# A hybrid Mamba, expert and Performer block on one core: another order of the same operations on four engines

## The chip, the core and the metric

One core of one Trainium2 chip. TensorE (PE) multiplies matrices, VectorE (DVE), ScalarE (ACT) and GpSimd (POOL) work elementwise, SyncE (SP) issues the transfers. The metric is the time of one execution on the device, in microseconds (us); smaller is better.

## What is computed

Input x has 4 sequences of 1024 tokens with 256 features. Four stages follow each other, each a layer norm, a block and a residual addition. Cut to what matters:

```
x = x + mamba(layernorm(x))          # state s: 256 features x 32 numbers a sequence
    # s = clip(s * A + b_t * x_t, -10, 10);  y_t = sum(c_t * s);  1024 steps in a row
x = x + ffn(layernorm(x))            # 8 experts, relu, the two best weighted (FFN1)
x = x + performer_and_mlp(layernorm(x))   # causal linear attention, then a gelu MLP of 1024
x = x + ffn(layernorm(x))            # the same experts again (FFN2)
```

All of it is float32; the first layers of experts and MLP run as sums of products of a high and a low half.

## The kernel before

`front_part` makes the scan's operands for all tokens and is not touched. `main_part` then works in 16 chunks of 64 tokens a sequence. It is pipelined by hand: the function `step(i, c, late)`, which each engine has in a form of its own, does the scan of chunk i, and beside it Mamba's output, FFN1, attention and the start of the MLP for chunk c = i - 1, and the rest of the MLP and FFN2 for chunk late = i - 2. Each engine runs step(0), step(1), a loop over i = 2 to 15, and two steps that drain the pipeline, without a scan. An engine takes its work strictly in the order in which step calls it, and waits on semaphores. So the order of the calls is the schedule; no planner decides at run time.

The scan joins the engines. For each of 64 tokens ACT makes u(s) (line 928, `u_ring`, 8 slots: u(s) waits for scan step s - 8). DVE's scan_step multiplies the state by the decay (line 1626) and adds with clipping (line 1635), each in two halves; the state ring has 16 slots. PE's y(n) = scan_output(i, n) (line 1220) multiplies 8 finished states by `cblk`, which POOL's next_cblk fills (line 840); scan step 8n + 16 may not overwrite the ring before y(n).

Names that the prediction speaks of. PE: first_layer and mlp_first (line 1287, 12 products), second_layer and mlp_second (1300), tpose_set (1234, transposes; T_FFN1, T_ATT, T_WO, T_MLP, T_FFN2 name the set), features (1375), values (1382), turn_k (1397), scores (1408, 128 small products), from_states (1418), from_chunk (1428), new_states (1439), attention_out (1389), turn_y (the step's first transposes), mamba (1362). DVE: add_expert (1748), set_acc (1735), query_feature (1826), mask (1836), attended (1796 and 1799), add_states (1807), add_attention (1813), ln_stats (1659, 1662), low_half (1678), low_half_mlp (1684), gate_y (1760, the step's first work). ACT: relu (1035), gelu (1055), ln_apply (983), copy_set (992), copy_hi (1005), copy_comb (1042), spread_kv (1027), copy_y (1011). POOL: rstd_of (821 to 828), add_mlp_bias (872), add_attention (879). The last two are additions of 128x512 elements.

The end of a step is a chain: attention_out on PE, add_attention and ln_stats on DVE, add_attention and rstd_of on POOL, ln_apply on ACT, tpose_set(T_MLP) on PE, copy_hi on ACT, low_half_mlp on DVE, mlp_first on PE. The scan's end is another: the last scan step on DVE, y(7) on PE, copy_y on ACT, turn_y on PE, gate_y on DVE.

## Time and profile before

| | us |
|---|---|
| three runs, median (lowest to highest) | 1843.38 (1839.24 to 1846.09) |
| the profiled execution | 1845.13 |
| its span, first to last instruction | 1843.3 |
| PE busy (share) | 1693.8 (92%) |
| DVE busy | 1565.0 (85%) |
| ACT busy | 926.0 (50%) |
| POOL busy | 245.1 (13%) |

The profile is of one execution. What lies beside the span in it is 1.8 us. A busy PE counts matmuls whose ends are modelled, so a short wait can hide in a busy share; the starts of matmuls are exact. The text calls the stretch from one copy_y to the next a step.

### The profile page before, as it was taken

What the parts mean: (1) busy time and instruction counts of PE and PEld (TensorE: products, weight loads), DVE (VectorE), ACT (ScalarE), POOL (GpSimd) and SP (SyncE); (2) the same over time, 40 slices, a digit from 0 to 9 for tenths busy, and PEclk for the clock granted to TensorE, in tenths of its full rate; (3) what the DMA queues carried; (4) which work ended last, traced back from release to release, by engine and by line L of the source; (5) the groups of instructions that cost most, each with busy time, mean ns of one, the idle gap of its engine ahead of it and who ended that gap; (6) DMA issues with size and microseconds to landing.
All of it is one profiled execution on the core that took longest, in us unless ns stands there. A gap on an engine that the chain in (4) does not pass through costs nothing. (4 is left out here: it accounts for less than half of the span.)

```text
span 1843.3 us, 55933 instructions
## 1 busy us (share of the span) xinstructions
PE 1693.8 (92%) x16992; PEld 1422.4 (77%) x16992; DVE 1565.0 (85%) x5957; ACT 926.0 (50%) x2134; POOL 245.1 (13%) x515
## 2 busy tenths in 40 slices
PE   5774889999999999999999999999999999999987
PEld 3332668787887878787888878787878878787986
DVE  6589879899998989898999999898989999997522
ACT  4674445463645555554645555455536455554322
POOL 1011011111102011110102020111101020111000
PEclk9886879999999989998999999899989999999998
DMA  6885333242333333332433323332423333330000
GB/s 191 298 247 147 110 94 99 77 117 75 102 96 90 100 84 110 91 96 77 110 87 93 107 81 98 100 99 81 117 71 93 105 89 104 93 98 20 1 7 6
DMA packets 108425, 182.63 MB, mean 99 GB/s; under 512 B 45288, under 2 KB 71936, under 8 KB 107648
## 3 DMA queue, kind: packets, MB, share of 16 engines
q1 hardware_dynamic: 107232, 178.71, 33.9%
q8 instruction: 146, 2.39, 0.6%
q14 instruction: 119, 0.97, 0.2%
q10 hardware_dynamic: 928, 0.56, 0.1%
HBM read 161.35 MB, written 17.83 MB: 97 GB/s over the span
## 5 line engine op out<-in xcount | busy, mean ns | idle before, releaser
L1635 DVE CUSTOM_DVE_ANT_0 state<-decayed_state,u_ring 128x128 f32<-128x128 f32 x2048 | 522.3, 293 | 11.1 <-ACT u_ring L928 4.7
L1626 DVE TENSOR_TENSOR decayed_state<-state,decay 128x128 f32<-128x128 f32 x2048 | 508.1, 289 | 2.7 <-POOL m_rstd L813 1.2
L1300 PE MATMUL bank<-f_w_sb,hs_whole 128*128 128x256 f32 x2048 | 488.3, 382 | 0.6 <-DVE res L1748 0.6
L928 ACT ACTIVATE u_ring<-xrep,b_steps 128x256 f32<-128x256 f32 x1024 | 450.5, 503 | 52.5 <-DVE state L1635 46.0
L1300 PEld LDWEIGHTS bank<-f_w_sb,hs_whole 128*128 128x128 f32 x2048 | 374.2, 191 | 45.9 <-DVE res L1748 1.0
L1035 ACT ACTIVATE hs_whole<-bank,f_b_sb 128x256 f32<-128x256 f32 x512 | 214.1, 470 | 373.1 <-PE bank L1287 373.1
L1287 PE MATMUL bank<-late_fT_parts,f_w_hi 128*128 128x256 f32 x1024 | 187.6, 306 | 0.0
L1287 PE MATMUL bank<-fT_parts,f_w_hi 128*128 128x256 f32 x1024 | 179.5, 297 | 4.6 <-DVE fT_parts L1678 3.4
L1220 PE MATMUL bank<-state,cblk 128*32 128x256 f32 x2048 | 151.3, 423 | 16.4 <-DVE state L1635 16.4
L1287 PEld LDWEIGHTS bank<-fT_parts,f_w_hi 128*128 128x128 f32 x1024 | 142.5, 189 | 23.3 <-DVE fT_parts L1678 7.1
L1287 PEld LDWEIGHTS bank<-late_fT_parts,f_w_hi 128*128 128x128 f32 x1024 | 149.8, 194 | 11.8 <-issue 5.8
L1748 DVE SCALAR_TENSOR_TENSOR x<-bank,comb,x 128x256 f32<-128x256 f32 x256 | 111.6, 478 | 19.5 <-PE bank L1300 19.4
L1748 DVE SCALAR_TENSOR_TENSOR res<-bank,comb,res 128x256 f32<-128x256 f32 x256 | 111.7, 478 | 15.5 <-PE bank L1300 11.7
L1300 PE MATMUL bank<-m_w_sb,hs_whole 128*128 128x256 f32 x512 | 118.3, 379 | 0.0
L1220 PEld LDWEIGHTS bank<-state,cblk 128*32 128x32 f32 x2048 | 59.2, 117 | 75.4 <-issue 36.3
L1300 PEld LDWEIGHTS bank<-m_w_sb,hs_whole 128*128 128x128 f32 x512 | 94.9, 190 | 11.6
L879 POOL TENSOR_TENSOR mb<-mb,a_t 128x512 f32<-128x512 f32 x16 | 20.5, 1279 | 608.2 <-DVE a_t L1813 608.2
L992 ACT ACTIVATE turn<-bank 128x512 f32<-128x512 f32 x48 | 28.6, 595 | 136.5 <-PE bank L1234 136.5
L821 POOL TENSOR_TENSOR m_ve<-m_mv,m_eps 128x2 f32<-128x2 f32 x96 | 20.7, 216 | 562.7 <-DVE m_mv L1662 562.7
L1287 PE MATMUL bank<-late_fT_parts,m_w_hi 128*128 128x256 f32 x512 | 91.4, 301 | 0.0
L1287 PE MATMUL bank<-late_fT_parts,f_w_lo 128*128 128x256 f32 x512 | 83.1, 286 | 0.0
L1287 PE MATMUL bank<-fT_parts,f_w_lo 128*128 128x256 f32 x512 | 81.0, 281 | 0.0
(157 smaller groups left out, 2296.3 us busy)
## 6 DMA issues: line engine op xcount, KB each, us to landing
xrep<-xs_dram SPq DMA_DIRECT2D x1024, 128.0 KB, 2.6
xt<-in_x SPq DMA_DIRECT2D x4, 1024.0 KB, 7.7
xn_dram<-xn SPq DMA_DIRECT2D x4, 1024.0 KB, 5.6
xs_dram<-xs SPq DMA_DIRECT2D x8, 512.0 KB, 4.4
f_w_sb<-in_f_w SPq DMA_DIRECT2D x2, 2048.0 KB
z_dram<-zT SPq DMA_DIRECT2D x8, 512.0 KB, 4.5
z_t<-z_dram SPq DMA_DIRECT2D x64, 64.0 KB, 2.3
out<-x SPq DMA_DIRECT2D x64, 64.0 KB, 2.1
```

What stands on the lines that cost most here:

```text
L821: pool.tensor_tensor(ve[:, k], mv[:, k, :, 1], eps[:, k], ALU.add).then_inc(ve_done[k].sem, 1)
L879: pool.tensor_tensor(mb[:], mb[:], a_t[:], ALU.add).then_inc(mb_done.sem, 1)
L928: act.activation(u_ring[:, s % USLOTS], xrep[:, slot, n], ACT.Copy, scale=b_steps[:, s // BSTEPS, s % BSTEPS:s % BSTEPS + 1]).then_inc(u_m ...
L992: act.activation(whole[:].rearrange("p k q -> p (k q)"), (HB[1] if k == T_WO else TB)[:], ACT.Copy).then_inc(tcopied[k].sem, 1)
L1035: act.activation(hs_whole[:, e % 2, m], hidden_bank(c, f, e)[:, m * TOK:(m + 1) * TOK], ACT.Relu, bias=g["f_b1"][:, e, m:m + 1]).then_inc( ...
L1220: last = pe.matmul(Y[YCOLS * j:YCOLS * (j + 1), tile * D:(tile + 1) * D], cblk[:, slot * YCOLS:(slot + 1) * YCOLS], state[:, s % RING, :], ...
L1287: last = pe.matmul(dst(tile), *((w_, d_) if stationary == "w" else (d_, w_)), start=first and stationary != "more", stop=(n == len(PRODUCT ...
L1300: last = pe.matmul(bank_[:, tile * D:(tile + 1) * D], hs_whole[:, slot, m, tile * P:(tile + 1) * P], w(m), start=(m == 0 and tile == 0 and ...
L1626: dve.tensor_tensor(decayed_state[:, part], state[:, (s - 1) % RING, part], decay[:, part], ALU.mult).then_inc(decayed.sem, 1)
L1635: dve._custom_dve(add_sat, out=state[:, s % RING, part], in0=decayed_state[:, part], in1=u_ring[:, s % USLOTS, part], s0=LIMIT, s1=-LIMIT) ...
L1748: dve.scalar_tensor_tensor(out=dst[:, tile], in0=out_bank(c, f, e)[:, tile * D:(tile + 1) * D], scalar=comb[:, f, tile, e:e + 1], in1=dst[ ...
```

## The change

The diff moves calls and adds or removes none; every engine issues the same operations, SP's part is untouched. The functions themselves do not change. Its core, where "..." marks what is left out:

```diff
@@ POOL
                 add_to_tokens()
                 rstd_of(c, MAMBA)
                 rstd_of(c, FFN1)
+                rstd_of(late, FFN2)
+                rstd_of(c, OUTER)
+                add_mlp_bias()
                 next_cblk(0)
                 next_cblk(1)
-                rstd_of(late, FFN2)
+                rstd_of(c, LN1)
                 next_cblk(2)
-                rstd_of(c, OUTER)
-                add_mlp_bias()
                 next_cblk(3)
-                rstd_of(c, LN1)
                 next_cblk(4)
+                next_cblk(5)
                 add_attention()
                 rstd_of(c, LN2)
-                next_cblk(5)
                 next_cblk(6)
@@ ACT
                 u(2)
                 u(3)
                 u(4)
+                gelu(late, 1)
                 u(5)
                 u(6)
                 u(7)
-                gelu(late, 1)
                 u(8)
                 u(9)
+                gelu(late, 2)
                 u(10)
+                gelu(late, 3)
                 u(11)
-                gelu(late, 2)
-                u(12)
-                gelu(late, 3)
                 ln_apply(c, FFN1, res, turn, xf_done[0])
                 copy_hi(c, T_FFN1)
                 copy_set(c, T_FFN1)
+                u(12)
                 u(13)
                 u(14)
+                u(15)
                 relu(c, 0, 0)
-                u(15)
+                u(16)
                 relu(c, 0, 1)
                 copy_comb(c, 0)
-                u(16)
-                relu(c, 0, 2)
                 u(17)
                 u(18)
                 u(19)
                 ln_apply(late, FFN2, x3, late_turn, xf_done[1])
...
                 u(48)
                 u(49)
                 u(50)
                 u(51)
-                relu(late, 1, 6)
                 u(52)
                 u(53)
                 u(54)
...
                 u(58)
                 u(59)
+                relu(late, 1, 6)
                 u(60)
+                spread_kv(c)
                 u(61)
                 u(62)
+                u(63)
                 relu(late, 1, 7)
                 ln_apply(c, LN2, a_t, late_turn, yl_done)
-                u(63)
-                spread_kv(c)
                 copy_hi(c, T_MLP)
@@ PE
                 first_layer(c, 0, 1)
                 if_both(x3_done, late, 1)
                 second_layer(c, 0, 0)
-                first_layer(c, 0, 2)
                 turn_comb(c, 0)
                 second_layer(c, 0, 1)
                 bias(c, 0)
-                y(1)
-                first_layer(c, 0, 3)
+                first_layer(c, 0, 2)
                 if_both(acc_set[0], c, 1)
                 tpose_set(late, T_FFN2, xf_done[1])
+                first_layer(c, 0, 3)
                 second_layer(c, 0, 2)
                 gate(late, 1)
+                second_layer(c, 0, 3)
                 first_layer(c, 0, 4)
-                second_layer(c, 0, 3)
+                y(1)
                 first_layer(c, 0, 5)
                 second_layer(c, 0, 4)
+                first_layer(c, 0, 6)
+                second_layer(c, 0, 5)
                 turn_comb(late, 1)
-                second_layer(c, 0, 5)
-                first_layer(c, 0, 6)
-                bias(late, 1)
                 first_layer(c, 0, 7)
                 second_layer(c, 0, 6)
+                second_layer(c, 0, 7)
                 if_both(relued[0], c, F // P * (E - 1))
                 first_layer(late, 1, 0)
-                second_layer(c, 0, 7)
+                y(2)
+                if_both(acc_done[0], c, TILES * (E - 1))
+                second_layer(late, 1, 0)
                 if_both(relued[0], c, F // P * E)
                 first_layer(late, 1, 1)
-                if_both(acc_done[0], c, TILES * (E - 1))
-                second_layer(late, 1, 0)
-                y(2)
-                y(3)
+                bias(late, 1)
                 first_layer(late, 1, 2)
                 if_both(acc_done[0], c, TILES * E)
                 second_layer(late, 1, 1)
+                y(3)
                 first_layer(late, 1, 3)
                 second_layer(late, 1, 2)
                 if_both(acc_set[1], late, 1)
                 tpose_set(c, T_ATT, xl_done)
                 second_layer(late, 1, 3)
-                first_layer(late, 1, 4)
                 if_both(relued[1], late, F // P * 2)
                 pe.wait_ge(tcopied[T_ATT].sem, tcopied[T_ATT].after(c, 1))
                 features(g["wk"], k_made)
-                second_layer(late, 1, 4)
-                first_layer(late, 1, 5)
                 values()
-                pe.wait_ge(kT_done.sem, kT_done.after(c, 1))
-                features(g["wq"], q_made)
+                first_layer(late, 1, 4)
                 pe.wait_ge(kT_done.sem, kT_done.after(c, 1))
                 pe.wait_ge(v_copied.sem, v_copied.after(c, TILES))
                 turn_k()
+                pe.wait_ge(kT_done.sem, kT_done.after(c, 1))
+                features(g["wq"], q_made)
+                second_layer(late, 1, 4)
+                first_layer(late, 1, 5)
                 y(4)
                 pe.wait_ge(qT_done.sem, qT_done.after(c, 2))
                 pe.wait_ge(k_copied.sem, k_copied.after(c, 1))
...
                 pe.wait_ge(masked.sem, masked.after(c, 3))
                 pe.wait_ge(kv_set.sem, kv_set.after(c, 0))
                 from_states()
+                y(5)
                 wait_apart(masked, masked.after(c, GH))
                 from_chunk(0)
                 from_chunk(1).then_inc(num_made.sem, 1)
                 new_states(0).then_inc(kv_half.sem, 1)
+                tpose_set(c, T_WO, at_done, HB[1])
                 wait_apart(kv_half, kv_half.after(c, 1))
                 new_states(1).then_inc(kv_made.sem, 1)
-                tpose_set(c, T_WO, at_done, HB[1])
-                y(5)
                 pe.wait_ge(tcopied[T_WO].sem, tcopied[T_WO].after(c, 1))
                 attention_out()
                 second_layer(late, 1, 6)
                 first_layer(late, 1, 7)
                 y(6)
+                second_layer(late, 1, 7)
                 pe.wait_ge(kv_added.sem, kv_added.after(c, 1))
                 tpose_set(c, T_MLP, yl_done)
-                second_layer(late, 1, 7)
                 y(OCTS - 1)
                 if late is not None:
                     pe.wait_ge(relued[1].sem, relued[1].after(late, E * (F // P)))
@@ DVE
                         first_layer_low(n)
                 mamba_norm()
                 ln_stats(c, FFN1, res, x1_done, (1, 2))
-                scan(5, 11)
+                scan(5, 10)
+                add_mlp()
                 if c is not None and late is None:
                     mlp_low()
                 low_half(c, T_FFN1)
-                add_mlp()
+                ln_stats(late, FFN2, x3, x3_done, (1, 1))
+                scan(10, 11)
+                routing(c, 0)
                 scan(11, 14)
-                routing(c, 0)
-                ln_stats(late, FFN2, x3, x3_done, (1, 1))
-                scan(14, 16)
                 set_acc(c, 0, res, res)
-                scan(16, 17)
+                scan(14, 15)
                 add_expert(c, 0, 0, res)
+                scan(15, 17)
+                add_expert(c, 0, 1, res)
                 scan(17, 18)
-                add_expert(c, 0, 1, res)
-                scan(18, 19)
                 add_expert(c, 0, 2, res)
+                scan(18, 21)
                 routing(late, 1)
-                scan(19, 22)
+                scan(21, 22)
                 add_expert(c, 0, 3, res)
-                scan(22, 23)
+                scan(22, 27)
                 add_expert(c, 0, 4, res)
-                scan(23, 25)
                 low_half(late, T_FFN2)
-                scan(25, 29)
                 add_expert(c, 0, 5, res)
+                scan(27, 28)
+                add_expert(c, 0, 6, res)
+                scan(28, 29)
+                add_expert(c, 0, 7, res)
                 scan(29, 30)
-                add_expert(c, 0, 6, res)
-                scan(30, 31)
-                add_expert(c, 0, 7, res)
                 ln_stats(c, OUTER, res, acc_done[0], (TILES * (E - 1) + 1, TILES * E))
-                scan(31, 32)
+                scan(30, 32)
+                ln_apply(c, OUTER, res, a_t, a_done)
+                scan(32, 33)
                 set_acc(late, 1, x3, x3)
-                ln_apply(c, OUTER, res, a_t, a_done)
+                scan(33, 34)
                 ln_stats(c, LN1, a_t, a_done, (1, 2))
-                scan(32, 35)
+                scan(34, 35)
                 add_expert(late, 1, 0, x3)
                 ln_affine(LN1, a_t, "ln1_s", lambda tile: rows["ln1_b"][:], turn, xl_done)
                 add_expert(late, 1, 1, x3)
                 scan(35, 37)
                 add_expert(late, 1, 2, x3)
-                scan(37, 38)
+                scan(37, 39)
                 add_expert(late, 1, 3, x3)
-                scan(38, 42)
+                scan(39, 40)
                 key_feature()
-                scan(42, 43)
-                add_expert(late, 1, 4, x3)
-                scan(43, 44)
+                scan(40, 44)
                 query_feature(0)
                 query_feature(1)
-                scan(44, 46)
+                scan(44, 45)
+                add_expert(late, 1, 4, x3)
+                scan(45, 47)
                 mask(0)
+                scan(47, 48)
                 mask(1)
                 mask(2)
-                scan(46, 47)
+                scan(48, 50)
                 mask(3)
-                scan(47, 51)
+                scan(50, 53)
                 add_expert(late, 1, 5, x3)
+                scan(53, 54)
                 attended()
-                scan(51, 57)
+                scan(54, 59)
                 add_states()
-                scan(57, 59)
+                scan(59, 60)
                 add_attention()
+                scan(60, 61)
                 ln_stats(c, LN2, a_t, xr_done, (1, 1))
-                scan(59, 61)
                 add_expert(late, 1, 6, x3)
                 scan(61, 64)
+                add_expert(late, 1, 7, x3)
                 low_half_mlp()
-                add_expert(late, 1, 7, x3)
 
             step(0, None, None)
             step(1, 0, None)
```

Three places in the order of the instructions. The first is PE's queue in the loop, from from_states (line 1418) to attention_out (1389); 1439 is new_states, 1234 the transposes T_WO, 1220 a y. Before:

```order
L1418 MATMUL bank<-kv,qT 64x68 x16
L1428 MATMUL bank<-vv,ss 64x17 x64
L1439 MATMUL bank<-vv,ktok 32x17 x64
L1234 MATMUL bank<-ident_sb,turn 128x128 x4
L1214 REGISTER_ALU
L1215 REGISTER_ALU
L1220 MATMUL bank<-state,cblk 32x256 x8
L1389 MATMUL bank<-wo_sb,turn 128x256 x4
```

and now:

```order
L1418 MATMUL bank<-kv,qT 64x68 x16
L1214 REGISTER_ALU
L1215 REGISTER_ALU
L1220 MATMUL bank<-state,cblk 32x256 x8
L1428 MATMUL bank<-vv,ss 64x17 x64
L1439 MATMUL bank<-vv,ktok 32x17 x32
L1234 MATMUL bank<-ident_sb,turn 128x128 x4
L1439 MATMUL bank<-vv,ktok 32x17 x32
L1389 MATMUL bank<-wo_sb,turn 128x256 x4
```

y(5) has moved ahead of from_chunk, and the transposes of the attended values stand between the two halves of new_states.

The second is PE's queue at the end of the loop's body, from y(6) to y(7). Before:

```order
L1220 MATMUL bank<-state,cblk 32x256 x8
L1234 MATMUL bank<-ident_sb,late_turn 128x128 x4
L1321 REGISTER_ALU
L1322 REGISTER_ALU
L1300 MATMUL bank<-f_w_sb,hs_whole 128x256 x4
L1214 REGISTER_ALU
L1215 REGISTER_ALU
L1220 MATMUL bank<-state,cblk 32x256 x8
```

and now:

```order
L1220 MATMUL bank<-state,cblk 32x256 x8
L1321 REGISTER_ALU
L1322 REGISTER_ALU
L1300 MATMUL bank<-f_w_sb,hs_whole 128x256 x4
L1234 MATMUL bank<-ident_sb,late_turn 128x128 x4
L1214 REGISTER_ALU
L1215 REGISTER_ALU
L1220 MATMUL bank<-state,cblk 32x256 x8
```

The last expert's second layer now stands ahead of the transposes T_MLP, not behind them.

The third is ACT's queue at the end of step(1), which has the loop's order without the work of the late chunk. From T_WO's copy (992) on, 928 is u, 983 ln_apply, 1027 spread_kv, 1005 copy_hi, 1011 copy_y. Before:

```order
L992 ACTIVATE turn<-bank 128x512
L928 ACTIVATE u_ring<-xrep,b_steps 128x256 x6
L983 ACTIVATE late_turn<-a_t,m_shift,m_rstd 128x256 x2
L928 ACTIVATE u_ring<-xrep,b_steps 128x256
L1027 ACTIVATE kv<-kv_sum 32x16x17 x4
L1005 ACTIVATE late_fT_parts<-bank 128x512
L1011 ACTIVATE turn<-bank 128x512
```

and now:

```order
L992 ACTIVATE turn<-bank 128x512
L928 ACTIVATE u_ring<-xrep,b_steps 128x256 x4
L1027 ACTIVATE kv<-kv_sum 32x16x17 x4
L928 ACTIVATE u_ring<-xrep,b_steps 128x256 x3
L983 ACTIVATE late_turn<-a_t,m_shift,m_rstd 128x256 x2
L1005 ACTIVATE late_fT_parts<-bank 128x512
L1011 ACTIVATE turn<-bank 128x512
```

spread_kv has left its place between the normed rows and their high halves, and the last u stands ahead of ln_apply.

## Rows read from the trace of the kernel before

**Rows 1.** The page: span, busy time of each engine, a DMA queue (packets, MB, share)

```profile
span 1843.3 us, 55933 instructions
PE 1693.8 (92%) x16992; PEld 1422.4 (77%) x16992; DVE 1565.0 (85%) x5957; ACT 926.0 (50%) x2134; POOL 245.1 (13%) x515
...
q8 instruction: 146, 2.39, 0.6%
```

**Rows 2.** Busy time by window: stretch, length, engines, granted clock (PEclk), DMA

```profile
158.70:261.50 102.80, 71.76 (x781) 55.85 (x781) 89.80 (x337) 43.59 (x100) 14.46 (x26) 0.73 0.34 91
261.50:1690.40 1428.90, 1382.53 (x14505) 1190.27 (x14506) 1312.32 (x5095) 746.23 (x1780) 202.87 (x420) 0.96 0.33 93
1690.40:1843.30 152.90, 133.80 (x1164) 121.39 (x1164) 53.86 (x142) 40.20 (x92) 12.83 (x26) 0.93 0.03 7
1388.50:1489.00 100.50, 97.13 (x1037) 83.61 (x1038) 93.83 (x365) 53.33 (x128) 14.52 (x30) 0.98 0.36 97
1077.90:1182.90 105.00, 100.33 (x1037) 86.11 (x1038) 93.93 (x365) 53.13 (x128) 14.43 (x30) 0.95 0.32 92
...
1474.00:1480.80 6.80, 6.80 (x41) 4.73 (x38) 6.48 (x30) 2.99 (x7) 0.00 (x0) 0.75 0.28 83
```

**Rows 3.** Timeline of PE, end of the step at 1388.5: start, length, instructions, [idle before]

```profile
1468.14 3.91 PE L1428 MATMUL bank<-vv,ss 64*64 64x17 f32 x128
...
1473.97 1.10 PE L1234 MATMUL bank<-ident_sb,turn 128*128 128x128 f32 x4
1475.00 1.94 PE L1220 MATMUL bank<-state,cblk 128*32 128x256 f32 x16
1476.87 2.26 PE L1389 MATMUL bank<-wo_sb,turn 128*128 128x256 f32 x8
1478.96 1.89 PE L1300 MATMUL bank<-f_w_sb,hs_whole 128*128 128x256 f32 x8
...
1482.20 1.07 PE L1220 MATMUL bank<-state,cblk 128*32 128x256 f32 x16
1485.53 0.63 PE L1234 MATMUL bank<-ident_sb,late_turn 128*128 128x128 f32 x4 [2.26 <-ACT late_turn L983]
```

**Rows 4.** Timeline of DVE, end of the same step

```profile
1472.11 0.37 DVE L1796 RECIPROCAL rec<-bank 128x16 f32<-128x16 f32 x2 [0.85 <-PE bank L1428]
...
1473.07 0.48 DVE L1626 TENSOR_TENSOR decayed_state<-state,decay 128x128 f32<-128x128 f32 x2
...
1476.40 0.49 DVE L1626 TENSOR_TENSOR decayed_state<-state,decay 128x128 f32<-128x128 f32 x2
...
1478.03 0.50 DVE L1635 CUSTOM_DVE_ANT_0 state<-decayed_state,u_ring 128x128 f32<-128x128 f32 x2 [0.32 <-DVE decayed_state L1626]
...
1480.46 0.68 DVE L1813 TENSOR_TENSOR a_t<-bank,a_t 128x512 f32<-128x512 f32 x1
...
1482.15 0.80 DVE L1626 TENSOR_TENSOR decayed_state<-state,decay 128x128 f32<-128x128 f32 x2
...
1488.14 0.69 DVE L1684 TENSOR_TENSOR late_fT_parts<-bank,late_fT_parts 128x512 fp32r<-128x512 f32 x1 [0.66 <-ACT late_fT_parts L1005]
...
1491.09 1.31 DVE L1760 TENSOR_TENSOR z_t<-bank,z_t 128x128 f32<-128x128 f32 x4 [1.47 <-PE bank L1234]
```

**Rows 5.** Timeline of POOL and ACT, the same stretch

```profile
1481.31 1.28 POOL L879 TENSOR_TENSOR mb<-mb,a_t 128x512 f32<-128x512 f32 x1 [37.02 <-DVE a_t L1813]
...
1485.69 1.80 ACT L1027 ACTIVATE kv<-kv_sum 32x272 f32<-32x272 f32 x4
```

**Rows 6.** Timeline of PE and DVE, two waits earlier in that step

```profile
1406.78 0.74 PE L1287 MATMUL bank<-fT_parts,f_w_hi 128*128 128x256 f32 x4 [0.34 <-DVE fT_parts L1678]
...
1460.53 1.53 DVE L1826 TENSOR_SCALAR qT<-bank,feature_floor_sb,feature_eps_sb 128x512 f32<-128x512 f32 x2 [1.42 <-PE bank L1375]
```

**Rows 7.** Timeline of PE in scores and behind them, step at 1077.9

```profile
1155.43 0.44 PE L1408 MATMUL bank<-qT,kT 32*64 32x64 f32 x18 [2.46 <-issue]
...
1157.91 2.92 PE L1300 MATMUL bank<-f_w_sb,hs_whole 128*128 128x256 f32 x8
```

More of the change, by code:

```diff
@@ L1108, in step @@
                 ln_apply(late, FFN2, x3, late_turn, xf_done[1])
+                relu(c, 0, 2)
                 copy_set(late, T_FFN2)
@@ L1115, in step @@
                 u(23)
+                relu(c, 0, 5)
                 u(24)
-                relu(c, 0, 5)
-                copy_comb(late, 1)
                 u(25)
                 u(26)
-                copy_hi(late, T_FFN2)
                 u(27)
@@ L1125, in step @@
                 u(29)
+                copy_hi(late, T_FFN2)
+                copy_comb(late, 1)
                 u(30)
+                u(31)
                 relu(c, 0, 7)
-                u(31)
                 u(32)
+                relu(late, 1, 0)
                 u(33)
-                relu(late, 1, 0)
                 u(34)
@@ L1137, in step @@
                 u(38)
+                u(39)
                 relu(late, 1, 2)
-                u(39)
                 u(40)
+                u(41)
                 relu(late, 1, 3)
+                u(42)
                 copy_set(c, T_ATT)
-                u(41)
-                u(42)
                 u(43)
+                copy_v(c)
                 u(44)
                 relu(late, 1, 4)
-                copy_v(c)
+                copy_k(c)
                 u(45)
                 u(46)
+                u(47)
                 relu(late, 1, 5)
-                copy_k(c)
-                u(47)
                 u(48)
```

## The prediction

> **What bounds the kernel now.** I read the page first, then the windows by step, then the timelines of one step. The page has PE busy for 92% of the span and DVE for 85% [rows 1], which does not yet say which of them decides. The windows do: the 14 steps from 261.5 to 1690.4 take 1428.9 us, 102.06 each, and PE is busy in 1382.5 of these, DVE in 1312.3 [rows 2]. Two engines are nearly full, so a step is as long as the work of either plus the waits that they cause each other. The step at 1388.5 takes 100.5, that at 1077.9 takes 105.0 [rows 2]; four of the 14 are like the second (104.1 to 105.0), ten like the first (100.3 to 102.3). The 4.5 us between the two come out of rows 7, to which I return. Step 1 before the loop and the drain behind it, 102.8 and 152.9 us, are not like this: PE is busy in 71.8 of the first, DVE in 53.9 of the second [rows 2].
>
> In the timeline of the shorter kind PE waits 2.26 us for T_MLP's rows behind y(6), and 0.34 for the low half in the first expert layer [rows 3, 6]. DVE waits 1.42 in query_feature, 0.85 in attended, 0.32 in the scan step behind it that needs y(5)'s place in the ring, 0.66 in low_half_mlp, 1.47 in gate_y [rows 4, 6]. From 1474.0 to 1480.8 the granted clock averages 0.75 [rows 2], full speed in one half and 1.2 GHz in the other: y(5) takes 1.94 in it, y(6) behind it 1.07 [rows 3]. Ahead of that PE did scores, from_states and from_chunk, hundreds of products of 17 to 68 columns.
>
> **The change, part by part.** Nothing is added or removed, and neither SP nor any DMA moves; ACT and POOL are busy for half and an eighth of the time [rows 1]. So only waits can change, and what runs beside what. I cost one loop step and multiply by 14.
>
> *The middle of the step, up to attended.* On DVE the scan steps 51 to 53 go ahead of attended. A scan step costs 0.83 (four from 1473.07 to 1476.40 [rows 4]), so 2.5 us of work go where DVE idled 1.42 + 0.85 = 2.27. On PE, y(5) goes ahead of from_chunk, 1.0 at full clock, while the 0.34 wait goes, since low_half runs a scan step earlier with add_mlp (0.6) in its place, and the small wait of scores for the queries goes, since k and q now come ahead of two expert layers. PE has the experts' layers to work on there, and I find no new wait over a few tenths: each second_layer's bank was freed by an add_expert that DVE reaches in time. So attended starts within half a microsecond of where it was; I book 0 for the middle. What would hurt is scores becoming later; then mask(0) waits on DVE.
>
> *The end on DVE.* From the first scan step behind attended to gate_y it is 1473.07 to 1491.09, 18.0 us [rows 4]. Three scan steps go, -2.5. The wait of 0.32 goes, since y(5) is long done. The wait of 0.66 goes: copy_hi stood behind spread_kv's 1.80 on ACT [rows 5] and now does not, and add_expert(7) fills the time. Against it stands POOL: its add_attention runs 1.28 us from 1481.31 [rows 5], and the pair of L1626 that starts beside it takes 0.80 where its neighbour takes 0.48 [rows 4]. It now has scan(60, 61) beside it from its first moment, where it had ln_stats. I charge the whole 1.28 less the 0.32 paid already, +0.96, as the row shows the DVE pair ending only with POOL's; the other end is 0. Sum: -2.5 - 0.32 - 0.66 + 0.96 = -2.5. gate_y's own wait of 1.47 stays, since y(7), copy_y and turn_y still follow the last scan step.
>
> The Trainium skill ("SBUF — State Buffer", section "SBUF: two separate sides") has GpSimd and a VectorE operation with two SBUF inputs share one port pair as an exclusive lock, with the loser blocked for the whole instruction. It speaks against this change, and L1626's 0.80 agrees with it. Without that rule this part would be -3.5 a step.
>
> *The end on PE.* From from_chunk's end (1468.14 + 3.91) to turn_y the same stretch of 18 us holds y(5) and the wait of 2.26. y(5) leaves: -1.9 here, +1.0 in the middle. second_layer(late, 1, 7), some 1.7 long, now covers the wait: -1.7. The first layer's 0.34 goes too. Sum: -2.9. But where y(5) and waits lay under the half clock, attention_out and second_layer(6) now come. At the slow clock a second_layer takes 2.92 instead of 1.89 [rows 3, 7], so each of the two may cost 1.0 more: between -0.9 and -2.9.
>
> *The step.* Both chains must come round, so the later one counts. DVE's is -2.5, PE's -0.9 to -2.9. I take **-2.4**, near DVE's, as attention_out was partly under the slow clock already (2.26 for the work of 1.89). 14 x 2.4 = 33.6. In step 1 PE has room and DVE's end gains the same waits, but it is one step: 0 to 2.5, I take 0. In the drain there is no scan, PE is busy in 133.8 of 152.9 and orders of experts change nothing: 0. The profiled execution took 1845.1; 1845.1 - 33.6 = 1811.5. The median of the three runs is 1.7 lower, so **1810**.
>
> **The longer steps.** In the step at 1077.9 scores stops after 110 of its 128 products for 2.46 us, "issue": no semaphore was awaited. Behind it products run at the slow clock [rows 7]. Queue q8 carried 146 packets, 2.39 MB, 16 KB each [rows 1]; that is 9 or 10 in a step, and PE has some 2075 products and weight loads in one [rows 2]. I read this as loading of code: scores issues 256 instructions in 1.5 us. The number and kind of instructions ahead of scores in the loop is unchanged, with y(4) still just ahead, so the block border falls at the same product; I leave four such steps as they are. The Trainium skill ("Runtime: NRT & Kernel Launch", section "Instruction fetch mechanics") has such blocks of 16 KiB mostly hidden, the next being fetched during the current one. By that no step would be long, before or after; the row of 2.46 says otherwise.
>
> **The rivals.**
> - *Dense and unstalled.* The clock's slow stretch falls no worse than before, the port costs nothing, and chance lets the stops of scores go away: -3.3 x 14 = -46, and four times 4.5 = -18 more. That is 1779; with half of the stops 1788. The waits in the rows speak for it, the four long steps against it. Its near end is 1797.
> - *The slow clock eats the gain.* It lasts longer, as work with few columns (from_states, y(5), from_chunk, new_states, transposes) now stands closer together, and attention_out, second_layer(6) and first_layer(7) all run slow. Then PE gains 0.3 a step or so: 1843.4 - 4 = 1839. For it: clock 0.75 in the same place; against it: y(5), which has 256 columns a product, comes into the thin stretch.
> - *Scores stops in every step: slower.* The place is between y(4) and scores. The queries now come earlier, so scores follows y(4) without its small wait, and there are a few tenths less for the code to arrive. Each stop costs 4.5, and up to 5.4 where no wait behind it (part of the 2.26) takes it up. Without stops the time would be 1843.4 - 18 - 34 = 1792; with 14 of them at 5.4, 1868. It decides from about 10 of 14 steps on (10 x 5.4 = 54 against the 52 of both gains). For it: the stop exists; against it: ten steps of 14 don't have it, with the same code.
> - *The change doesn't do what it says*: the three places of the order show that it does; no chance of its own.
>
> **How the numbers follow.** Forecast 0.68, its own range 1797 to 1829 (3.3 and 1.0 a step). Dense and unstalled 0.10, slow clock 0.12, stops in every step 0.10. A measurement of this kernel can tell about 0.5%, 9 us, from no change. Faster: 0.68 + 0.10 = 0.78; within: 0.12; slower: 0.10. The range goes from 1788, half of the stops gone, to 1846, the slow clock with a few more stops; it leaves out the last rival and a piece of the first.
>
> **What would show it.** Steps of 97.5 to 98.5 us between copies of y, four or so longer; idle PE before the T_MLP transposes under 0.5; no wait in low_half_mlp; no wait of 1.42 in query_feature, and instead up to 1 us before the first mask; POOL's L879 with a long L1626 beside it. It is wrong if from_chunk ends over 1 us later in the step than 83.6, if L1408 shows an issue wait in most steps, or if the clock is slow for over 7 us behind from_chunk.

## Result and the profile after

The changed kernel takes 1817.18 us (median of 4 runs, 1816.62 to 1818.00), against 1843.72 before: ratio 0.986, 95% interval 0.984 to 0.988. That is 7 us above the forecast of 1810 and inside its range. The page:

```profile
span 1814.9 us, 55933 instructions
PE 1689.0 (93%) x16992; PEld 1416.7 (78%) x16992; DVE 1580.4 (87%) x5957; ACT 933.3 (51%) x2134; POOL 246.6 (14%) x515
```

The windows of step 1, of the 14 loop steps, of the drain and of the ordinary step at 1065.5, to set beside [rows 2]; the columns are the same:

```profile
159.50:267.50 108.00, 72.40 (x781) 56.29 (x782) 90.73 (x337) 44.63 (x100) 14.25 (x26) 0.72 0.31 87
267.50:1663.60 1396.10, 1377.25 (x14505) 1184.83 (x14506) 1326.76 (x5096) 752.30 (x1779) 204.62 (x420) 0.97 0.34 95
1663.60:1814.90 151.30, 133.11 (x1164) 120.70 (x1164) 53.62 (x141) 40.41 (x92) 12.82 (x26) 0.95 0.03 7
1065.50:1165.30 99.80, 98.88 (x1037) 85.00 (x1038) 94.90 (x365) 53.72 (x128) 14.62 (x30) 0.97 0.35 97
```

The loop gives 1428.9 - 1396.1 = 32.8, nearly the 33.6 of the forecast, but not from where the forecast had it. Ordinary steps went from 100.5 to 99.7, only 0.8 and not 2.4. Here 100.5 is an undisturbed step of before, like those at 977.4 and 1388.5; the median over its ten steps without a stop is 100.8, and against that it is 1.1. The long steps of 104 to 105 are gone: the longest of the 14 is the first, 100.5, all others lie within 99.5 to 99.9. Step 1 grew from 102.8 to 108.0.

That the long steps are gone shows in what PE's idle time in front of scores' products and their weight loads was put down to. The changed kernel (us, times), where the 5.8 are 0.41 ahead of the first product of each loop step and none is inside scores:

```profile
  issue: 5.8, 14
  DVE qT L1826: 1.7, 2
```

and the kernel before, same view:

```profile
  issue: 29.6, 23
  DVE qT L1826: 7.2, 18
```

PE's timeline of the step at 1065.5, from scores to turn_y, beside [rows 3]:

```profile
1139.17 1.59 PE L1408 MATMUL bank<-qT,kT 32*64 32x64 f32 x128
...
1145.13 1.07 PE L1220 MATMUL bank<-state,cblk 128*32 128x256 f32 x16
1146.14 3.91 PE L1428 MATMUL bank<-vv,ss 64*64 64x17 f32 x128
...
1153.23 3.78 PE L1389 MATMUL bank<-wo_sb,turn 128*128 128x256 f32 x8
1156.81 2.08 PE L1300 MATMUL bank<-f_w_sb,hs_whole 128*128 128x256 f32 x8
...
1160.21 1.07 PE L1220 MATMUL bank<-state,cblk 128*32 128x256 f32 x16
1161.60 1.99 PE L1300 MATMUL bank<-f_w_sb,hs_whole 128*128 128x256 f32 x8 [0.33 <-DVE x L1748]
1163.43 0.61 PE L1234 MATMUL bank<-ident_sb,late_turn 128*128 128x128 f32 x4
```

y(5) takes 1.07 at the full clock where it took 1.94 at the half, and the wait of 2.26 for T_MLP's rows is gone. attention_out takes 3.78 where it took 2.26: the granted clock is 0.50 from 1150.40 to 1157.20.

```profile
1150.40:1157.20 6.80, 6.43 (x112) 5.19 (x102) 6.31 (x29) 3.97 (x10) 0.00 (x0) 0.50 0.24 72
```

The same step on DVE, from the last mask to gate_y, and POOL's add_attention beside it:

```profile
1145.11 0.68 DVE L1836 TENSOR_TENSOR ss<-bank,causal_sb 128x512 f32<-128x512 f32 x1
...
1150.10 0.37 DVE L1796 RECIPROCAL rec<-bank 128x16 f32<-128x16 f32 x2 [0.20 <-PE bank L1428]
...
1153.55 0.49 DVE L1635 CUSTOM_DVE_ANT_0 state<-decayed_state,u_ring 128x128 f32<-128x128 f32 x2 [0.34 <-ACT u_ring L928]
...
1158.07 1.57 DVE L1635 CUSTOM_DVE_ANT_0 state<-decayed_state,u_ring 128x128 f32<-128x128 f32 x2
...
1164.76 0.68 DVE L1684 TENSOR_TENSOR late_fT_parts<-bank,late_fT_parts 128x512 fp32r<-128x512 f32 x1
1167.39 1.01 DVE L1760 TENSOR_TENSOR z_t<-bank,z_t 128x128 f32<-128x128 f32 x3 [1.95 <-PE bank L1234]
```

```profile
1157.91 1.38 POOL L879 TENSOR_TENSOR mb<-mb,a_t 128x512 f32<-128x512 f32 x1 [18.09 <-DVE a_t L1813]
```

The pair of L1635 takes 1.57 beside POOL, where a pair takes 0.51. The waits in low_half_mlp (0.66) and in query_feature (1.42) are gone, gate_y's grew from 1.47 to 1.95.

**A way to cut a step.** For the experiments a step is cut at attended (L1796): from copy_y to attended, and the rest up to the next copy_y. All times but the last two columns count from the step's first copy_y. The rows are medians over the 14 loop steps, here and in the table further down, except that before has its undisturbed steps (977.4 and 1388.5):

| kernel | scores starts | attended | rest | step |
|---|---|---|---|---|
| before | 73.7 | 83.6 | 16.85 | 100.5 |
| changed | 73.7 | 84.6 | 14.90 | 99.7 |

So the new end gives 1.95 and the way up to attended takes 1.0 of it back. Against the medians of before's ten steps without a stop (attended 83.9, step 100.8) the way up to attended takes 0.7.

### The profile page after: what moved, and what is told of

The parts are those of the page before. It is cut to its first block and busy times, and to the rows that moved or that the text cites. A ratio compares the mean times of both kernels' runs of the same rounds, so it can differ in the third digit from the quotient of the medians.

```text
span 1814.9 us, 55933 instructions
## 1 busy us (share of the span) xinstructions
PE 1689.0 (93%) x16992; PEld 1416.7 (78%) x16992; DVE 1580.4 (87%) x5957; ACT 933.3 (51%) x2134; POOL 246.6 (14%) x515
## 5 line engine op out<-in xcount | busy, mean ns | idle before, releaser
L1635 DVE CUSTOM_DVE_ANT_0 state<-decayed_state,u_ring 128x128 f32<-128x128 f32 x2048 | 552.9, 308 | 18.2 <-ACT u_ring L928 10.5
L1287 PE MATMUL bank<-late_fT_parts,f_w_hi 128*128 128x256 f32 x1024 | 181.1, 299 | 0.1
L1220 PE MATMUL bank<-state,cblk 128*32 128x256 f32 x2048 | 142.2, 396 | 19.3 <-DVE state L1635 13.7
L1287 PEld LDWEIGHTS bank<-late_fT_parts,f_w_hi 128*128 128x128 f32 x1024 | 145.3, 190 | 11.1 <-issue 5.8
L1748 DVE SCALAR_TENSOR_TENSOR res<-bank,comb,res 128x256 f32<-128x256 f32 x256 | 111.5, 478 | 11.0 <-PE bank L1300 10.2
L1220 PEld LDWEIGHTS bank<-state,cblk 128*32 128x32 f32 x2048 | 54.9, 111 | 67.9 <-issue 26.7
L1055 ACT ACTIVATE hs_whole<-bank,m_b_sb 128x256 f32<-128x256 f32 x128 | 53.5, 469 | 77.6 <-PE bank L1287 77.6
```

The lines of the kernel that those rows point to most:

```text
L1055: act.activation(hs_whole[:, j % 2, m], HB[j % 2][:, m * TOK:(m + 1) * TOK], ACT.Gelu_apprx_tanh, bias=g["m_b1"][:, 2 * j + m:2 * j + m + ...
L1220: last = pe.matmul(Y[YCOLS * j:YCOLS * (j + 1), tile * D:(tile + 1) * D], cblk[:, slot * YCOLS:(slot + 1) * YCOLS], state[:, s % RING, :], ...
L1287: last = pe.matmul(dst(tile), *((w_, d_) if stationary == "w" else (d_, w_)), start=first and stationary != "more", stop=(n == len(PRODUCT ...
L1635: dve._custom_dve(add_sat, out=state[:, s % RING, part], in0=decayed_state[:, part], in1=u_ring[:, s % USLOTS, part], s0=LIMIT, s1=-LIMIT) ...
L1748: dve.scalar_tensor_tensor(out=dst[:, tile], in0=out_bank(c, f, e)[:, tile * D:(tile + 1) * D], scalar=comb[:, f, tile, e:e + 1], in1=dst[ ...
```

## Experiments

There are twelve kernels in three groups: e1 to e4; r1 and e5 to e7; e8 to e11. Before ran beside each group: 1833.68 (1824.62 to 1849.44, 23 runs), 1848.12 (1842.79 to 1860.40, 7) and 1842.97 (1831.67 to 1859.03, 19). It scatters by over 1%, the changed kernel by 0.1%; so totals are compared within a group, and where the text goes across groups it says so. Steps are compared by their profiles, one execution of each kernel.

### The parts of the change alone

e1: middle on PE (and its counterparts on DVE and ACT, copy_k ahead of relu(5)); before:

```diff
-                first_layer(late, 1, 4)
...
                 features(g["wk"], k_made)
-                second_layer(late, 1, 4)
-                first_layer(late, 1, 5)
                 values()
...
-                features(g["wq"], q_made)
+                first_layer(late, 1, 4)
...
                 turn_k()
...
+                features(g["wq"], q_made)
+                second_layer(late, 1, 4)
+                first_layer(late, 1, 5)
                 y(4)
```

> The kernel before with the middle of the new order alone: on PE the queries' features, second_layer(4) and first_layer(5) stand between turn_k and y(4), on DVE the queries come ahead of add_expert(4) and scan steps stand between the masks, on ACT copy_k comes ahead of relu(5). Theory A: the long steps come from code that arrives too late behind y(4); with an expert's two layers ahead of y(4) PE's fetch starts over 1 us earlier relative to scores, so no step has an issue wait in L1408, and ordinary steps keep 100.5, since scores starts where it did (PE bound). Total 1843.4 - 4 x 4.5 - some 2 for the smaller ones = 1823 to 1826. Rival B: the stops come and go by chance or hang on the end of the step; then three or more long steps of 104 to 105 remain and the time is 1839 to 1846.

e2: the end, from from_states on, as in the diff of the change.

> The kernel before with the end of the new order alone: y(5) ahead of from_chunk, T_WO between the halves of new_states, second_layer(7) ahead of T_MLP, scan steps 51 to 53 ahead of attended, (60) beside POOL's add_attention, add_expert(7) ahead of low_half_mlp, and ACT's and POOL's moves that go with them. Theory A: ordinary steps fall from 100.5 to 99.6 (attended 0.95 later because of y(5), the end 1.8 shorter), the long steps stay, four or so, step 1 grows by 2 to 5: 1843.4 - 12 + 3 = 1834. Rival B: it is the end that takes the long steps away: 1816 to 1820.

e3: both.

> Middle and end together; against the changed kernel only the head of the step (up to the transposes T_ATT) stays as before. Theory A: the head is worth nothing, so 1817 +- 3, with no long step, ordinary steps of 99.6 and step 1 near 108. Rival: the head gives the part that the other two do not, 1823 or more here.

e8: e1 with the masks together:

```diff
                 mask(0)
-                scan(47, 48)
                 mask(1)
                 mask(2)
-                scan(48, 50)
+                scan(47, 48)
                 mask(3)
-                scan(50, 51)
+                scan(48, 51)
```

> The kernel before with the middle of e1, but the masks together again (0, 1, 2, one scan step, 3). Theory A: e1 lost 1.0 a step because mask(3) comes 1.3 later and from_chunk waits for it, and gained the stops; so here attended is back near 83.3, ordinary steps 100.0 to 100.4, no stop inside scores: 1843 - 18 - 4 and, with step 1, about 1822 to 1828. Rival B: e1's loss is the thin work at the half clock that begins earlier; then ordinary steps stay over 101 and the time near 1838.

| kernel | median us (runs) | steps stopped in scores | scores | attended | rest | step |
|---|---|---|---|---|---|---|
| e1 middle | 1843.42 (10) | 0 of 14 | 73.3 | 84.8 | 16.85 | 101.5 |
| e2 end | 1828.17 (10) | 1 | 73.6 | 85.2 | 14.90 | 100.2 |
| e3 both | 1809.79 (4) | 0 | 73.3 | 84.2 | 14.90 | 99.3 |
| e8 middle, masks together | 1823.89 (4) | 0 | 73.2 | 83.2 | 16.85 | 100.3 |

Against before beside them, e1 is 10 us slower, e2 6 and e3 24 faster, and e8 is 19 faster.

Three readings. The rest is 16.85 wherever the old end stands and 14.90 wherever the new one does: the end's gain adds up. The stops go with the middle: none in e1, e3 and e8. In e2's profile one is left, at the same product as in [rows 7]:

```profile
1341.36 1.44 PE L1408 MATMUL bank<-qT,kT 32*64 32x64 f32 x110 [0.26 <-DVE qT L1826]
1345.53 0.68 PE L1408 MATMUL bank<-qT,kT 32*64 32x64 f32 x18 [2.73 <-issue]
```

And the middle alone is no gain in total (1843): it takes the stops away but attended comes 1.2 later. My expectation of e1 was wrong by 18 us there, though right on the stops. The reason stands in its timeline: the scan steps between the masks make mask(3) late, and from_chunk waits 0.74. The granted clock then averages 0.82 from 1060.90 to 1065.50, and from_chunk takes 4.57 instead of 3.91.

```profile
1059.00 1.17 PE L1418 MATMUL bank<-kv,qT 128*64 128x68 f32 x32
1060.90 4.57 PE L1428 MATMUL bank<-vv,ss 64*64 64x17 f32 x128 [0.74 <-DVE ss L1836]
```

e8 confirms it: with the masks together from_chunk starts 0.8 earlier in the step than in e1 and, at the faster clock, ends 1.6 earlier; attended is at 83.2, and the total 20 us less (in another group). In the loop windows e3 is 5.2 us below the changed kernel, and it has the old head, so the head of the new order gains nothing and costs about 0.35 a step (scores at 73.3 against 73.7). e5 and e7, further down, differ by this head alone, within one group: 1813.85 with it, 1805.46 without.

```profile
267.56:1658.50 1390.94, 1368.27 (x14505) 1185.19 (x14506) 1322.69 (x5096) 750.77 (x1779) 205.02 (x420) 0.97 0.34 96
```

### What y(5) ahead of from_chunk does

```diff
                 from_states()
-                y(5)
                 wait_apart(masked, masked.after(c, GH))
                 from_chunk(0)
                 from_chunk(1).then_inc(num_made.sem, 1)
+                y(5)
                 new_states(0).then_inc(kv_half.sem, 1)
```

> The changed kernel with y(5) moved back behind from_chunk, one call. Theory A: y(5) fills the wait for mask(3) (0.74 in e1) at the full clock; behind from_chunk it runs at the half clock (1.87 instead of 1.00) and on the way to T_WO, attended is at most 0.3 earlier: ordinary steps 100.4 to 101.0, total 1828 to 1836. Rival B: y(5) ahead of from_chunk is a plain delay of 1.0 on the way to attended, as its 84.55 against 83.60 looks; then each step gets shorter by 0.5 to 1.0 and the total is 1803 to 1810.

e9 takes 1838.69 (1836.32 to 1840.75, 10 runs), with steps of 101.7 and some of 100.3; the changed kernel, in the group before, takes 1817.16. That is theory A's direction, some 3 us beyond its end; rival B is out. The rows show both halves of it, the wait and the half clock, which here lasts 10.2 us and in the changed kernel's loop steps at most 6.8:

```profile
1057.59 4.20 PE L1428 MATMUL bank<-vv,ss 64*64 64x17 f32 x128 [0.73 <-DVE ss L1836]
1061.71 1.93 PE L1220 MATMUL bank<-state,cblk 128*32 128x256 f32 x16
```

```profile
1061.00:1071.20 10.20, 10.20 (x176) 7.59 (x174) 7.87 (x34) 5.39 (x13) 0.00 (x0) 0.50 0.21 54
```

Attended is even 0.3 later without y(5) in front. With the masks spaced as here, y(5) is not a delay of 1.0; it fills a wait that the spacing makes. Where they stand together it is one: in e2 the last mask ends 78.6 into the step, as in before, and from_chunk starts at 80.6 instead of 79.6. So two things hold from_chunk back to 80.6 in the changed kernel, and either would do nearly all of it: y(5), and a last mask that ends at 80.3. Masks together and y(5) behind from_chunk, with the rest of the new end, was not run.

### Where the stops in scores come from

e4 and e10 leave work and order of before as they are and shift code. At the top of the loop body:

```diff
+                if late is not None:
+                    for _ in range(40):
+                        pe.wait_ge(pool_set.sem, POOL_SETS)
                 turn_y()
```

> The kernel before, with 40 waits on a semaphore that has long had its value at the top of PE's loop body: work and order the same, but PE's code from there on lies 40 instructions further back. Theory A (code arrival): the place where scores stopped moves 20 products forward, to about product 90, and the fetch for what lies behind it is asked for 40 instructions earlier in the work, over 1 us earlier; the long steps go, 1823 to 1828 if the 40 waits cost nothing (they may cost up to 1 us a step, up to 14 more). Rival B (the stop belongs to scores itself or to chance): products stop at 110 as before, four long steps.

and the same with 16 waits on DVE ahead of gate_y:

> The kernel before with 16 waits that are long satisfied at the top of DVE's loop body, where DVE waits for PE anyway: the code of DVE lies 16 instructions further back. It tells what makes PE's fetch come 2.5 late in some steps. Rival C (a clash of the two fetches: in every step of before another queue's fetch lands at 71.4, 0.7 ahead of PE's at 72.1): with that one shifted no step stops, all times of the kernel within 1822 to 1827. Theory A (PE's own lead alone): stops as in before, its times as far apart as those of before, up to 1845.

e4 takes 1854.73 (8 runs), e10 1844.96 (1828.35 to 1854.89, 10 runs). In e4 no loop step stops, neither behind 110 products nor behind 90; its 40 waits cost 1.7 a step, more than I had allowed, so its total says nothing for the theory and its trace does. In e10 seven of 14 steps stop, behind 110 products each, though the fetch of the other queue (q14) moved from 71.4 to 70.3: rival C is out.

```profile
1158.90 1.44 PE L1408 MATMUL bank<-qT,kT 32*64 32x64 f32 x110 [0.26 <-DVE qT L1826]
1162.80 0.68 PE L1408 MATMUL bank<-qT,kT 32*64 32x64 f32 x18 [2.46 <-issue]
```

The packets of queue q8 tell the rest. In ordinary steps of before (the loop's first left out) one starts 72.0 to 72.3 into the step, 1.5 ahead of scores. In the stopping step at 1077.9 there is none; the transfers from 1149.90 to 1152.40 (72.0 to 74.5 into the step), then from 1152.40 to 1153.00:

```profile
DMA packets 0, 0.00 MB, mean 0 GB/s; under 512 B 0, under 2 KB 0, under 8 KB 0
```

```profile
q8 instruction: 1, 0.02, 16.2%
```

It starts at 74.6, when scores is at work already. Where an expert's layers stand ahead of y(4), as in e1 (its window 1051.00 to 1052.00 holds the packet, at 70.7), it starts 2.5 ahead of scores:

```profile
q8 instruction: 1, 0.02, 7.0%
```

| | fetch starts ahead of scores, typically | loop steps that stopped |
|---|---|---|
| before, e2, e10 | 1.5 | 4, 1 and 7 of 14 each |
| changed, e1, e3, e5 to e9, e11 | 2.5 | 0 of 140 with the repeat of the changed kernel |
| e4 | 6.5 | 0 of 14 |

The typical value is that of steps without a stop. In the second line two steps have a lead of only 1.7, and they don't stop either.

So a stop goes with a late fetch, and the lead is set by what stands ahead of y(4) (e1) or by where the code lies (e4). That q8 brings PE's code is inferred from this. Why the fetch with the short lead starts 2.5 later in some steps and not in others stays open; no run tells it. The Trainium skill ("Runtime: NRT & Kernel Launch", section "Instruction fetch mechanics") has the next block fetched while the current one runs, mostly hidden. In scores that holds for the 154 steps of the last two lines and not for 12 of 42 in the first.

### The port

```diff
                 add_attention()
-                scan(60, 61)
                 ln_stats(c, LN2, a_t, xr_done, (1, 1))
+                scan(60, 61)
                 add_expert(late, 1, 6, x3)
```

> The changed kernel with DVE's ln_stats(LN2) ahead of scan step 60 again, one swap. Theory A (port): the pair beside POOL's add_attention no longer waits it out (1.89 to 0.83 for the step, some 0.3 stays as in before), and LN2's mean comes 1.9 earlier, so T_MLP too: 0.5 to 0.8 a step, 7 to 11 below the changed kernel. Rival B: PE sets the end of the step, what DVE saves is waited for at gate_y: within 2 of the changed kernel.

e6 takes 1806.07 (1802.65 to 1807.10, 4 runs), against 1817.16 of the changed kernel beside it: 11 less, and 0.69 a step (rest 14.46, step 99.0). The pair beside POOL now takes 0.81, and second_layer(7) stands behind y(6) without a wait:

```profile
1053.74 0.81 DVE L1626 TENSOR_TENSOR decayed_state<-state,decay 128x128 f32<-128x128 f32 x2
```

```profile
1055.09 1.07 PE L1220 MATMUL bank<-state,cblk 128*32 128x256 f32 x16
1056.09 1.99 PE L1300 MATMUL bank<-f_w_sb,hs_whole 128*128 128x256 f32 x8
```

This is theory A, at the upper end of its size; PE did not hold the gain back.

### Step 1, and all together

r1 is the changed kernel again, e5 the changed kernel with this in all four engines' step functions, where the first branch holds the body in the order of before, the second the new one:

```diff
+                if late is None:
...
+                else:
...
```

> The changed kernel itself again, as the measure for the three beside it. Both theories: 1817 +- 3, no issue wait inside scores in any loop step, PE's fetch at 71.0 and scores at 73.65 in the step.

> The changed kernel with step(0) and step(1), which have no late chunk, in the order of before on all four engines; the loop and the drain as changed. Theory A: step 1 is a chain of latencies with idle engines, and y(5) ahead of from_chunk, the scan steps between the masks and (60, 61) lie on that chain: step 1 falls from 107.9 to 102.8 and the stretch ahead of it by 0.8, total 5 to 6 below the changed kernel. Rival: step 1's growth comes from the head of the loop's first step or from the clock and only moves; the sum of step 1 and step 2 falls by less than 2.

> Middle and end of the new order in the loop and drain, the head as before, and step(0) and step(1) all as before. Additive: the run with middle and end (1809.8) less 5 to 6: 1804. Rival: the head of the changed kernel is worth as much as on a par, then no lower than e5.

> What the runs point to, together: middle and end of the new order, head as before, step(0) and step(1) as before, ln_stats(LN2) ahead of scan step 60. Additive from e7 (1805.5) and e6 (-0.66 a step, -11 in all): 1795 to 1797, ordinary steps 98.6. Rival: the two gains meet at PE, whose own work then fills the step: 1801 or more.

r1 takes 1817.16, e5 1813.85, e7 1805.46 and e11 1800.02 (4 runs each, none more than 3.1 from its median). e5 is 3.3 below r1, and e7 4.3 below e3 (in another group): the direction of theory A, two thirds of its size. Step 1 of one kernel isn't constant: it takes 108.0 in the first profile of the changed kernel, 105.2 in the second; 102.8 in before's, and 105.2 in e10's, whose step 1 is before's; 104.6 in e5's. What e5 and e7 lack of the forecast lies in scores at least in part: in step 1 it stops for 1.4 and 1.7, 116 products in. before's profile has no such stop; those of e4, e10 and e11, with the same step 1, have it. In before's the fetch starts 1.4 ahead of scores there, in these five 0.5 behind its start. So step 1 shows the same as the loop. PE is at rest for a third of step 1. As the changed kernel has it:

```profile
240.37 2.08 PE L1418 MATMUL bank<-kv,qT 128*64 128x68 f32 x32 [3.54 <-DVE ss L1836]
242.38 1.94 PE L1220 MATMUL bank<-state,cblk 128*32 128x256 f32 x16
244.24 7.01 PE L1428 MATMUL bank<-vv,ss 64*64 64x17 f32 x128
...
264.45 1.09 PE L1234 MATMUL bank<-ident_sb,late_turn 128*128 128x128 f32 x4 [6.22 <-ACT late_turn L983]
```

and as before had it:

```profile
236.42 1.17 PE L1418 MATMUL bank<-kv,qT 128*64 128x68 f32 x32 [1.98 <-DVE ss L1836]
237.94 6.67 PE L1428 MATMUL bank<-vv,ss 64*64 64x17 f32 x128 [0.36 <-DVE ss L1836]
```

Here the scan steps between the masks (a wait of 3.54 for the mask instead of 1.98), and y(5) at the half clock, stand ahead of from_chunk with no other work to hide them. e11 is the best version: 0.977 of before (0.970 to 0.985), 17 us below the changed kernel of the group before. It misses the additive 1796 by 4: ordinary steps are 98.9, not 98.6. PE is busy in 1373.8 of the loop's 1384.2, so the rival (the gains meet at PE) may have a share in it; no run shows that.

```profile
263.99:1648.16 1384.17, 1373.82 (x14505) 1190.72 (x14506) 1312.33 (x5096) 750.35 (x1780) 209.00 (x420) 0.97 0.34 96
```

## Why the prediction was right, and where not

The total was right, and in part by luck: the ordinary steps gave 11 us of the 34 booked, and steps that the forecast left as they are gave 22. Each part in turn:

- **The middle, booked at 0: wrong.** Attended comes 1.0 later. The 0.34 and the wait of scores for the queries did go, but scores starts at 73.7 as before (the head costs 0.35). So nothing paid for y(5)'s 1.0 ahead of from_chunk, and the masks with scan steps between them end 1.7 later, which alone would hold from_chunk back nearly as long. I had looked for a later scores, not for a later mask(3); the second is what e1 showed.
- **The end on DVE, -2.5: from the first scan step behind attended to gate_y it went from 18.0 to 16.3, -1.7.** Three scan steps left it, as booked. The 0.66 went. The port cost the pair 1.57 - 0.51 = 1.06, where the forecast had 1.28; less the 0.32 that before paid already it is 0.74, against the 0.96 of the forecast. So the rule of the Trainium skill ("SBUF — State Buffer", "SBUF: two separate sides") held, and e6, which got 0.69 a step back, agrees with the size. The 0.32 did not go, and I had read it wrongly: it stands ahead of scan step 56 in both kernels (median 0.32 in each), though in the changed one y(5) was done 7 us before it, and u(56), which ACT makes ahead of T_WO's copy, 8.6 us before it. So it isn't y(5)'s, nor u's, though the view puts it down to u_ring; its cause stays open (ACT's rows stand below). And gate_y's wait, "stays", grew by 0.5: without it DVE's stretch got 2.2 shorter, and PE's, which turn_y ends, only 1.7.
- **The end on PE, -0.9 to -2.9: at its weak end.** That sum holds y(5)'s +1.0 in the middle and the 0.34 of the head. From from_chunk's end to turn_y it went from 18.3 to 16.6, -1.7; with these two it is -1.0. In the two steps shown, by the starts of the groups: y(5) -1.9, y(6) with the wait behind it -1.9; against that, at the half clock, attention_out +1.5 and second_layer(6) +0.2, and new_states and T_MLP +0.2 each. I had allowed up to 1.0 for each of attention_out and second_layer(6), and together they took 1.7 of the 2.0. "The later one counts", I wrote, and then took DVE's -2.4, for which PE would have had to come near its good end. The step shortened by 1.95 (copy to copy) less 1.0.
- **The four long steps, "left as they are": wrong.** They took 104.7 on average, 17 us above four undisturbed ones; together with smaller hitches of the other steps of before, which are gone too and which no run explains, it is 21.8. I argued that the number of instructions ahead of scores had not changed, so neither had the block border. The number is indeed the same, 1055 from turn_y to scores in both traces; where the border falls can't be seen where nothing stops. But what counts is how long before scores PE reaches the place at which the fetch is asked for, and the two expert layers put there made that 1.0 more. I had even written, as a rival, that less time would be left for the code; it is more.
- **Step 1, 0 to a gain of 2.5: wrong in sign**, +5.2 between the two profiles, 3 to 4 by e5 and e7. Drain: 1.6 less, booked at 0.
- Of the rivals, the stops of scores went away as in the first one, but not by chance: 0 of 140. The slow clock, the second, took most of what the forecast had allowed it. The run's signs: no wait in low_half_mlp, none in query_feature, none of PE ahead of T_MLP, a wait of 0.41 before the first mask and the long pair beside L879 came as written; steps of 97.5 to 98.5 did not. from_chunk ends 84.56 into the step (median), just short of the mark that I had set for being wrong (84.6), and the half clock behind it lasts up to 6.8 us, just short of the 7 that I had set.

In us: ordinary shortening 14 x 0.8 = 11, the stops and smaller hitches of the other steps 21.8, step 1 -5.2, front and drain +0.8: 28.4 between the two spans.

ACT's rows in the step at 1065.5 for u(56) and, next in its queue, T_WO's copy; the wait of scan step 56 ends at 1153.55:

```profile
1144.39 0.51 ACT L928 ACTIVATE u_ring<-xrep,b_steps 128x256 f32<-128x256 f32 x1 [1.52 <-DVE state L1635]
1152.36 0.60 ACT L992 ACTIVATE turn<-bank 128x512 f32<-128x512 f32 x1 [7.46 <-PE bank L1234]
```

## What to carry to other kernels

Count what an order does to the slowest chain in the prologue too: an order that fills a full loop with other work delays the stages that have none to fill with. A burst of many small instructions needs its code early, and longer work ahead of it gave it here 1 us more; in a trace, compare where the fetch starts, not only how many instructions there are. And when single steps of a loop are longer than the rest, find their cause before pricing a change at the ordinary step.

## Not expected of the hardware

- A satisfied wait is not free: 40 of them on PE's queue cost 1.7 us a step, in a place where PE has no idle time in before.
- Kernels whose profiles show stops scatter in their times: with ten runs each, e2 spread over 20 us and e10 over 27, e1 over 7 and e9 over 4, which have none.
- In the stopping steps the fetch doesn't start a little late: leaving out each loop's first step, the 26 steps of before and e10 have it at 72.0 to 72.6 or at 74.5 to 75.4, and none between.
